# Last normalisation of a four-layer graph network: applied on ScalarE from a scale and a bias, with the output stored in three parts

## The reference

```
x = layernorm(x + L0(x));  x = layernorm(x + L1(x))
x = layernorm(x + L2(x));  x = layernorm(x + L3(x))
layernorm(x) = (x - mean(x)) / sqrt(var(x) + 1e-5)
```

## Time and profile before

| | us |
|---|---|
| three runs, median (lowest to highest) | 1367.52 (1365.2 to 1370.31) |
| the profiled execution, its own time | 1366.98 |
| its span, first to last instruction | 1365.2 |
| PE busy in the span | 1162.6 (85%) |
| DVE busy | 868.6 (64%) |
| ACT busy | 456.5 (33%) |
| POOL busy | 265.5 (19%) |
| mean granted TensorE clock | 0.924 |

### The profile page before, as it was taken

How to read it: one execution, slowest core, us unless ns; L and a number is a source line. 1 busy time by engine, 2 the same in 40 slices (tenths; PEclk the granted TensorE clock), 3 DMA queues, 4 the chain that set the end, 5 groups by cost and what they waited for, 6 DMA issues and landing times.

```text
span 1365.2 us, 15096 instructions
## 1 busy us (share of the span) xinstructions
PE 1162.6 (85%) x5730; PEld 885.8 (65%) x5730; DVE 868.6 (64%) x1536; ACT 456.5 (33%) x673; POOL 265.5 (19%) x313
## 2 busy tenths in 40 slices
PE   5987733668779998799999999999999999879983
PEld 2644511334458986698789877798779877636552
DVE  6676743456545266667766567767766567946885
ACT  1110640000013452246234353245234442215781
POOL 1147438888501001100110001100100001110001
PEclk9988876879889999799999999999999999778897
DMA  6236886312030231211110201112010220100001
GB/s 180 65 90 185 262 282 150 67 34 50 4 124 1 86 99 53 85 62 63 31 41 22 100 24 54 41 62 63 14 49 32 100 62 32 38 0 1 1 1 38
DMA packets 47904, 93.97 MB, mean 69 GB/s; under 512 B 17200, under 2 KB 17600, under 8 KB 46418
## 3 DMA queue, kind: packets, MB, share of 16 engines
q1 hardware_dynamic: 27338, 71.77, 16.5%
q0 software_dynamic: 20480, 20.99, 6.7%
HBM read 74.65 MB, written 17.91 MB: 68 GB/s over the span
## 4 chain that ended last, share of the span: by engine, by line
PE 64%; DVE 13%; POOL 9%; ACT 5%; issue 5%; DMA 3%; SPq 0%; POOLq 0%; DVEq 0%; ACTq 0%
PE ps L1522 15%; PE ps L1469 14%; PE ps L1497 10%; POOL logit_ring L588 6%; PE ps L1502 5%; PE ps L1656 4%; PE ps L1556 4%; POOL arena L582 3%; PE ps L1602 2%; DMA logits_scratch<-arena 2%; PE ps L1627 2%; PE ps L1485 2%; ACT arena L782 1%; PE ps L1508 1%; DVE arena L1421 1%
## 5 line engine op out<-in xcount | busy, mean ns | idle before, releaser
L1469 PE MATMUL ps<-arena 125*128 125x314 f32 (+5 forms) x820 | 225.3, 453 | 15.9 <-DVE neg_max L1028 11.8
L1469 PEld LDWEIGHTS ps<-arena 125*128 125x128 f32 (+5 forms) x820 | 142.1, 186 | 88.6 <-DVE neg_max L1028 17.0
L566 POOL TENSOR_TENSOR var_eps<-mean_var,ln_consts 125x1 f32<-125x1 f32 x70 | 15.6, 223 | 930.6 <-DVE mean_var L1175 565.2
L1627 PE MATMUL ps<-arena 125*125 125x512 f32 x192 | 122.7, 733 | 73.9 <-DVE arena L1057 58.2
L582 POOL DMA_INDIRECT arena<-value_scratch,src_idx x80 | 99.9, 1248 | 75.9 <-issue 33.2
L588 POOL DMA_INDIRECT logit_ring<-logits_scratch,pair_idx x80 | 106.1, 1326 | 24.4 <-issue 24.1
L1556 PE MATMUL ps<-ident,arena 125*125 125x125 f32 x625 | 81.1, 284 | 15.6 <-ACT arena L858 7.7
L1556 PEld LDWEIGHTS ps<-ident,arena 125*125 125x125 f32 x625 | 75.9, 195 | 25.1 <-ACT arena L858 8.9
L1627 PEld LDWEIGHTS ps<-arena 125*125 125x125 f32 x192 | 33.5, 219 | 76.2 <-issue 76.0
L1628 PEld LDWEIGHTS ps<-arena 125*125 125x125 f32 x192 | 41.0, 213 | 56.8 <-issue 56.8
L1497 PE MATMUL ps<-input_high,weight_high 128*128 128x314 f32 x320 | 72.9, 309 | 2.7 <-DVE weight_low L1159 2.7
(11 more groups left out here) (267 smaller groups left out, 2618.3 us busy)
## 6 DMA issues: line engine op xcount, KB each, us to landing
logits_scratch<-arena SPq DMA_DIRECT2D x5, 2187.5 KB
arena<-in_m_w SPq DMA_DIRECT2D x8, 1024.0 KB, 6.4
arena<-in_w_up SPq DMA_DIRECT2D x4, 1024.0 KB, 5.5
arena<-in_w_down SPq DMA_DIRECT2D x4, 1024.0 KB, 7.5
arena<-in_wq SPq DMA_DIRECT2D x4, 1024.0 KB, 5.3
arena<-in_wk SPq DMA_DIRECT2D x4, 1024.0 KB, 5.2
arena<-in_wv SPq DMA_DIRECT2D x4, 1024.0 KB, 5.1
arena<-in_wo SPq DMA_DIRECT2D x4, 1024.0 KB, 5.3
```

The costliest lines, as they stand in the source:

```text
L1469: last = mm(out_view[:, place:place + HALF_W], w, r[:, lo:lo + HALF_W], start=n == 0, stop=n == len(pairs) - 1 and not open_end)
L1627: mm(ps[0:TILE, 512 * j:512 * j + 512], onehot, VG[slot][:, u, :], start=False, stop=True, skip_group_check=True)
```

## The change

`norm` is no longer called for the last normalisation. DVE now does only `block3_end`, bn_stats and bn_aggr for each tile, with no `part_wait` between them, and no tensor_scalar. POOL computes rstd as before, and in addition mean x rstd (`centre`), and signals that. ACT negates `centre` into `shift`, waits for its own result, and applies the normalisation to the tile in place, X x rstd + shift, as one Identity activation with a scale and a bias from SBUF; this counts up `out_ready`. SP waits for `out_ready` three times (2, 4 and 5 tiles) and stores each group of tiles as soon as it is done, by two transfers each (partitions 0 to 111, partitions 112 to 124), six in all. The output is stored in the same 2 KB pieces as before. Two new SBUF tensors of 125 x 5 fp32 are allocated among the small ones.

```diff
--- before.py
+++ after.py
@@ -275,7 +275,9 @@
         mv = sbuf("mean_var", [TILE, NT, 2])
         rstd = sbuf("rstd", [TILE, NT])
         vare = sbuf("var_eps", [TILE, NT])
+        centre = sbuf("mean_rstd", [TILE, NT])
         lnc = sbuf("ln_consts", [TILE, 2])
+        shift = sbuf("minus_mean_rstd", [TILE, NT])
         negm = sbuf("neg_max", [TILE, 2, NT])
         psums = sbuf("prob_sums", [TILE, 2, NT])
         rinv = sbuf("prob_rinv", [TILE, 2, NT])
@@ -542,9 +544,11 @@
                 else:
                     sp.wait_ge(sig("x1_stored"), 32)
                     node_transfer(XIN, rows_view(x1_d), "ld_x1")
-            sp.wait_ge(sig("out_ready"), NT)
-            node_transfer(rows_view(out), X, "out_stored")
-            sp.wait_ge(sig("out_stored"), 32)
+            for pair in PAIRS:
+                sp.wait_ge(sig("out_ready"), pair[-1] + 1)
+                tiles = slice(pair[0], pair[-1] + 1)
+                node_transfer(rows_view(out)[:, tiles, :], X[:, tiles, :], "out_stored")
+            sp.wait_ge(sig("out_stored"), 32 * len(PAIRS))
 
         @block.gpsimd
         def _(pool):
@@ -626,8 +630,13 @@
                 powers((sig("var_ready1"), sig("rstd_ready1")), pool_chain, n * NT)
             B.wait_filled(pool, ("m1", LAYERS - 1, FT - 1))
             g.tensor_copy(PICKG, ident[0:2 * H3, H3:2 * H3].unsqueeze(2).to_broadcast([2 * H3, H3, TILE])).then_inc(sig("pick_ready"), 1)
-            for n in range(3):
+            for n in range(2):
                 powers((sig("var_ready3"), sig("rstd_ready3")), pool_chain, n * NT)
+            for t in range(NT):
+                pool.wait_ge(sig("var_ready3"), 2 * NT + t + 1)
+                pool_chain(pool, g.tensor_tensor(vare[:, t:t + 1], mv[:, t, 1:2], lnc[:, 0:1], ALU.add))
+                pool_chain(pool, g.tensor_tensor(rstd[:, t:t + 1], vare[:, t:t + 1], lnc[:, 1:2], ALU.pow))
+                g.tensor_tensor(centre[:, t:t + 1], mv[:, t, 0:1], rstd[:, t:t + 1], ALU.mult).then_inc(sig("centre_ready"), 1)
 
         @block.scalar
         def _(act):
@@ -878,6 +887,11 @@
                     exps3(h + 1)
                 if h + 2 < H3:
                     edge_sums(h + 2)
+            for t in range(NT):
+                act.wait_ge(sig("centre_ready"), t + 1)
+                a.activation(shift[:, t:t + 1], centre[:, t:t + 1], ACT.Copy, scale=-1.0).then_inc(sig("shift_ready"), 1)
+                act.wait_ge(sig("shift_ready"), t + 1)
+                a.activation(X[:, t, :], X[:, t, :], ACT.Identity, bias=shift[:, t:t + 1], scale=rstd[:, t:t + 1]).then_inc(sig("out_ready"), 1)
 
         @block.vector
         def _(dve):
@@ -1454,7 +1468,10 @@
                     B.wait_evacuated(dve, ("x", n))
                     dve_chain(dve, v.tensor_tensor(X[:, tiles, :], X[:, tiles, :], V[:, tiles, :], ALU.add))
 
-            norm(back, 2 * NT, X, block3_end, done=sig("out_ready"))
+            for t in range(NT):
+                block3_end(t)
+                dve_chain(dve, v.bn_stats(stats[:, t, :], X[:, t, :]))
+                v.bn_aggr(mv[:, t, :], stats[:, t, :]).then_inc(sig("var_ready3"), 1)
 
         @block.tensor
         def _(pe):
```

## The result

| us | before | after |
|---|---|---|
| median of 20 runs each (lowest to highest) | 1368.13 (1361.66 to 1375.36) | 1362.26 (1357.38 to 1364.66) |
| profiled execution, own time | 1366.98 | 1364.4 |
| its span | 1365.2 | 1362.2 |

What follows compares the result with a forecast made beforehand. The end's path was taken as DVE, POOL, DVE, then a store of all 1250 KB. Issuing the store 1.79 us earlier and 3.48 us less store gave 1367.52 - 5.27 = 1362.3 us, range 1360.2 to 1365.4.

Steps and rivals of the forecast that it cites:

- The 1.75 us: DVE, last normalisation: time saved by taking tensor_scalars off the path, 0.57, 0.43 and 0.75 us.
- the 0.55 us of the count: DVE, between bn_stats and bn_aggr: dropping part_wait saves 0.11 us in each of five tiles.
- the 0.75 of that tile: DVE, after tile 3's bn_aggr: L1450 could start at 1353.90 instead of 1354.65, 0.75 us earlier.
- 1.15 + 1.05 = 2.20 us: From the last bn_aggr's end: POOL takes 1.15 us to finish centre, then ACT's part takes 1.05.
- The activation: ACT's Identity instruction on a tile of 512 elements: 0.78 us, with bounds of 0.65 and 0.87.
- 0.02 + 2.89: After the last tile is done: SP's 0.02 us, then 2.89 us for the last part of the store, before 6.37.
- some 0.3 for POOL: POOL's queue: tiles 1 and 3 can wait some 0.3 us for POOL, tile 4 not.
- 2 (mutual exclusion on tile 4): DVE's L1455 of tile 4 waits for POOL's L567 of tile 3, 0.25 us later: 1362.6 us; chance 0.25.
- 3 (a dear last store): Last part of the store hardly shrinks with size, costing 4.2 us, not 2.89: 1363.6 us; chance 0.15.
- 4 (the hand-over eats the gain): ACT hand-over: out_ready complete no earlier than before, only the store's 3.48 us remain: 1364.0 us; chance 0.12.
- 5 (transfers in turn): Store: six transfers served one after another, 3.19 us each, slower than before at 1372.3 us; chance 0.03.
- 6: Anything else of the whole program, such as two small tensors shifting the others, in either direction; chance 0.07.

Runs made afterwards that it cites:

- e3: Kernel before without part_wait in the last normalisation: 17.82 us from its first bn_stats to the end of the span (end stretch), against 18.58 us before.
- e7: Changed kernel with the output stored in five parts, one per tile, by ten transfers: end stretch 13.05 us, against 13.27 in the changed kernel.
- e10: The kernel of e7 run again and timed: end stretch 13.13 us, ratio to the kernel before 0.9955.
- e4: Changed kernel with tile 4 alone normalised by DVE's tensor_scalar, store still in three parts: end stretch 13.59 us, last store 3.98 us, ratio 0.9961.
- e12: e4 with 24 one-element memsets added to DVE's stream: end stretch 13.18 us, last store 3.56 us.
- e6: Changed kernel with one more, wide POOL addition of two SBUF blocks at tile 3: end stretch 14.87 us, against 13.27 in the changed kernel.
- e1: Changed kernel with the output stored in one go after all five tiles, as before: end stretch 16.73 us, ratio 0.9988.
- e9: e4 with the output stored in five parts, one per tile: end stretch 13.42 us, last store 3.80 us.
- e11: e9 with 24 one-element memsets added to DVE's stream: end stretch 12.70 us, last store 3.08 us, ratio 0.9951.

## Why the prediction was right

The mechanism came as worked out, piece by piece, and one piece of it with luck. That the median itself is 1362.26 for a forecast of 1362.3 is luck too: single runs of the changed kernel scatter over 7 us, and the 20 runs of before have a median 0.61 us above that of the three from which the forecast started.

**DVE.** Forecast: last bn_aggr 8.20 us after the first bn_stats. Measured: 8.14. The 1.75 us are those of three tensor_scalars (the text says that tiles 0 to 3 each lose one from the path, but prices the fourth, rightly, at nothing); with the 0.55 us of the count they make 2.30, and 2.36 came. e3 shows that the second term was read rightly from one gap at another place. It also shows that the terms are not independent: without the count the kernel before gained 0.75, since the pause of the tensor_scalar behind tile 3 went too. In the forecast that pause was already within the 0.75 of that tile, and no tensor_scalar is left that could wait for POOL, so the sum stood.

**POOL and ACT.** Forecast 1.15 + 1.05 = 2.20 us from bn_aggr's end to "ready", measured 2.25: POOL 1.17, the hop 0.03, then 0.20, 0.04 and 0.81. The activation, priced at 0.78 between 0.65 and 0.87, took 0.81. The lower bound rests on a price for one operand that no row of this case gives.

**The last store.** Forecast 0.02 + 2.89 from "ready" on, measured 2.88; e7 and e10 place the undisturbed value at 2.7. The forecast was right here partly by luck. The text had tile 3 ready 8.1 us after the first bn_stats and its data over well before the last part's packets start; it was ready at 8.36 (1357.29). Most of the difference is a wait that the text had seen ("some 0.3 for POOL") and left out of the 8.1: tile 3's bn_aggr ended at 1354.80, and POOL, still on tile 2, took it up at 1355.12. Its data ended at about 1360.0, just ahead of the last part's, which began at about 1360.2. Against e7 and e10 that cost 0.1 to 0.2 us. Had the last tile been ready 0.8 us sooner, as in e4 and e12, the same sum would have been 0.7 to 1.1 us too low. The step that cost this queue at nothing had no margin, and the text did not say how much.

**Rivals.** 2 (mutual exclusion on tile 4) fell for this kernel, at 0.02 us, though the mechanism is real (e6). It was also priced too low by its own rule: with POOL's wait left out the text had POOL's power and L1455 overlap for 0.25 us, and in the trace they overlap for 0.53 (1355.41 to 1355.94), so a hold for the whole of the power would have cost twice the 0.25. 3 (a dear last store) fell for the change, 2.88 for 4.2; e4 shows what brings it about. 4 (the hand-over eats the gain) fell: e1 gained 1.85 us with ACT alone, against 1.79 forecast, and "ready" itself came 1.80 sooner (12.19 to 10.39). 5 (transfers in turn) fell: e7 has ten instead of six and is no longer. 6: no instruction ahead of the end was changed, and the runs' difference, 4.8 to 8.1 us, holds the 5.3 of the end stretch; whether something else adds to it these runs can't tell.

**The part of noise.** The last normalisation began between 1344.67 (e10) and 1353.78 (e3) over the profiled executions, 9.1 us apart, with the same work ahead of it. That is more than the change brings, and it is why single executions say nothing here and why the end stretch was used. Nearly all of it arises early. The 1400th matmul of the trace starts at 467.4 us in e10 and at 476.0 in e3, so 8.6 of the 9.1 us are there by then; for the kernel before and the changed one it is 470.2 and 472.4, 2.2 of their 2.31. What the early stages wait for differently was not looked into.

## What to carry to other kernels

At the end of this kernel only the last piece of output pays the store's fixed time (in the earlier trace rows, 0.87 us before the first packets and 0.70 after the last), so storing what is done early is worth nearly all of the transfer's length: 3.5 of 6.4 us here. But the pieces must be *ready* early: about 0.6 us of the gain came only because the step was taken off the engine whose order kept tile 3 behind tile 4's statistics. And a step saved ahead of the last transfer can be lost in it: look at what is in the queue, other parts and instruction transfers, in the microsecond around the last issue.

## What was not expected of the hardware

- A count on a semaphore in DVE's stream, between two instructions of which one waits for the other, cost 0.11 us each time (gap 0.15 with it, 0.04 without).
- An instruction transfer of about 0.01 MB on q14, tied to a place in DVE's program, lengthened the last part of the store by 0.4 to 0.7 us (e4 to e12, e9 to e11). It shows as one DMA engine's share, 0.07, after the others have finished.
- The pair of issues of the last part took SP 1.01 to 1.12 us when a part of two tiles had been issued only 1.2 us ahead, and 0.76 or 0.77 otherwise.
- A POOL product of one element per partition took 1.25 us instead of 0.19 beside an addition of DVE with both inputs in SBUF, and DVE's addition 1.52 instead of 0.71 behind a wide POOL instruction; a power of POOL over one element per partition, 0.55 us long, cost an addition of DVE that began 0.02 us after it only 0.02 us.
